# A two-layer transformer kernel on one core: an order planned in finer steps, a key projection moved ahead, and two copies moved from VectorE to ScalarE

## The reference, cut to what matters

```
x = x + L0_attn(layernorm(x))   # one head of 64, biases, causal softmax, output projection
x = x + L0_ffn(layernorm(x))    # 8-bit quantised x and weights, one 256 x 256 product, bias
x = x + L1_attn(layernorm(x))   # 16 heads of 16, rotary positions, causal softmax, projection
x = x + L1_ffn(layernorm(x))    # see below
```

```
xr = mu_r * x + (1 - mu_r) * x_prev
xk = mu_k * x + (1 - mu_k) * x_prev
out = sigmoid(xr @ W_r.T) * (square(relu(xk @ W_k.T)) @ W_v.T)
```

## Time and profile before

| | |
|---|---|
| median of 3 runs | 2519.56 us (2517.97 to 2519.94) |
| profiled execution | 2517.27 us |
| its span in the trace | 2514.1 us |
| PE busy | 2320.8 us (92%) |
| PEld busy | 1053.0 us (42%) |
| DVE busy | 1985.3 us (79%) |
| ACT busy | 1512.4 us (60%) |
| POOL busy | 525.7 us (21%) |
| mean granted clock of PE | 0.981 |

### The profile page before, as it was taken

One profiled execution on the slowest core, in us unless ns is written; L12 is line 12 of the kernel. 1 busy time (PEld: TensorE's weight loads), 2 busy tenths in 40 slices (PEclk: granted clock), 3 DMA queues, 4 the chain that ended last, 5 costly groups with the idle time before them and its releaser, 6 DMA issues.

```text
span 2514.1 us, 52353 instructions
## 1 busy us (share of the span) xinstructions
PE 2320.8 (92%) x19371; PEld 1053.0 (42%) x19371; DVE 1985.3 (79%) x4326; ACT 1512.4 (60%) x2753; POOL 525.7 (21%) x526
## 2 busy tenths in 40 slices
PE   8889899999999899998999999999999999999998
PEld 4544333333434335353444534344344434332345
DVE  5778689887787887879787787997788688899932
ACT  2234456575655666676675666657566577677762
POOL 5453210302215012120403303031121400000011
PEclk9899999999999999999999999999999999999999
DMA  2322220120211312021121302112021121110111
GB/s 56 83 72 73 76 58 25 38 59 18 83 34 35 82 43 73 15 79 29 42 65 37 91 19 76 40 35 78 12 76 35 42 70 45 31 42 27 28 37 36
DMA packets 185896, 125.41 MB, mean 50 GB/s; under 512 B 84912, under 2 KB 185392, under 8 KB 185648
## 3 DMA queue, kind: packets, MB, share of 16 engines
q1 hardware_dynamic: 184880, 121.16, 17.4%
q10 hardware_dynamic: 768, 0.92, 0.1%
HBM read 62.20 MB, written 59.24 MB: 48 GB/s over the span
## 4 chain that ended last, share of the span: by engine, by line
PE 55%; DVE 29%; ACT 6%; issue 4%; DMA 2%; SPq 2%; DVEq 1%; POOL 1%; POOLq 0%; ACTq 0%
DVE mx L1543 20%; PE psum L1867 12%; PE psum L1845 6%; PE psum L1812 6%; PE psum L1778 4%; ACT probs L1303 4%; PE psum L1742 3%; PE psum L1887 2%; PE psum L1713 2%; PE psum L1898 2%; PE psum L1651 2%; PE psum L1918 2%; PE psum L1799 2%; PE psum L1906 2%; DVE stats L1402 1%
## 5 line engine op out<-in xcount | busy, mean ns | idle before, releaser
L1303 ACT ACTIVATE probs<-psum 128x512 f32<-128x512 f32 x2176 | 1139.4, 607 | 465.8 <-PE psum L1845 310.2
L1543 DVE TENSOR_REDUCE mx<-psum 128x1 f32<-128x512 f32 (+2 forms) x2304 | 1283.4, 620 | 140.9 <-PE psum L1812 99.5
L1867 PE MATMUL psum<-probs,vs 128*17 128x512 f32 (+3 forms) x5120 | 590.7, 543 | 0.7 <-ACT probs L1303 0.3
L1812 PE MATMUL psum<-kst,qst 48*128 48x512 f16 (+3 forms) x2560 | 439.6, 354 | 71.0 <-DVE mx L1543 37.7
L1845 PE MATMUL psum<-qst,kst 50*128 50x512 f16 (+3 forms) x2560 | 428.7, 353 | 55.7 <-DVE mx L1543 19.5
L1812 PEld LDWEIGHTS psum<-kst,qst 48*128 48x128 f16 x2560 | 134.0, 94 | 397.5 <-DVE mx L1543 154.5
L1845 PEld LDWEIGHTS psum<-qst,kst 50*128 50x128 f16 x2560 | 128.2, 94 | 360.1 <-ACT probs L1303 131.4
L1867 PEld LDWEIGHTS psum<-probs,vs 128*17 128x17 f32 x5120 | 93.1, 96 | 155.5 <-issue 127.6
L1088 POOL TENSOR_SCALAR vare<-mv 128x4 f32<-128x4 f32 x64 | 15.5, 241 | 595.5 <-DVE mv L1405 595.5
L1819 PE MATMUL psum<-maskq,identh 64*128 64x128 bf16 (+1 forms) x2048 | 131.1, 205 | 0.0
L1117 POOL TENSOR_TENSOR sums<-probs 128x512 f32<-128x512 f32 x12 | 15.3, 1272 | 494.3 <-ACT probs L1257 494.3
(11 more groups left out here) (173 smaller groups left out, 2876.2 us busy)
## 6 DMA issues: line engine op xcount, KB each, us to landing
qk_dram<-parts SPq DMA_DIRECT2D x168, 128.0 KB
qst<-qk_dram SPq DMA_DIRECT2D x128, 96.0 KB, 2.3
kst<-qk_dram SPq DMA_DIRECT2D x128, 96.0 KB, 2.3
v_dram<-vst SPq DMA_DIRECT2D x64, 136.0 KB, 4.0
vs<-v_dram SPq DMA_DIRECT2D x64, 136.0 KB, 2.1
xs<-x_in SPq DMA_DIRECT2D x16, 512.0 KB, 3.5
x_dram<-xs SPq DMA_DIRECT2D x16, 512.0 KB, 2.9
att_dram<-ast SPq DMA_DIRECT2D x64, 128.0 KB, 2.0
```

The costliest lines, as they stand in the source:

```text
L1303: act.activation(dst, src, ACT.Exp, scale=DK1 ** -0.5 / LIFT ** 2).then_inc(S["exp"], 1)
L1543: ins = dve.tensor_reduce(mx1[:, n % 2, 2 * g + odd, tile % TPC, c:c + 1], bank(src, at, at + cols), AX.X, ALU.max)
L1812: ins = pe.matmul(two[odd][:, at:at + cols], qst[rows, qslot, pair, P * (tile % TPC):P * (tile % TPC + 1)], kst[rows, kslot, pair, 0:cols] ...
L1867: ins = pe.matmul(bank(7, off, CH, rows=VW, row=32 * h), vtile[:, h, :], probs[:, HG * (step_no(b, hg, k) % PSTEPS) + h, at:at + CH - off] ...
```

## The change

Four things change. The planner's stretch goes from 40 to 25 us and its drawings from 8 to 16, and each drawing is played to three stretches ahead (75 us) in place of two (80 us). In the tail, the mix for K comes before the mix for R, and K before R. The copy of the turned maxima, `turnmax d`, goes from DVE to ACT, with 0.2 us for it in the plan in place of 0.13. The copy of the first attention's values, `v0`, goes from DVE to ACT, with the same 0.4 us in the plan. Since every queue comes from the plan, the order of all the other work changes too.

```diff
-STRETCH, WAYS, MOVE = 40.0, 8, 10.0
+STRETCH, WAYS, MOVE = 25.0, 16, 10.0
...
-                self.go(trial, then, number, (at + 2) * STRETCH, weights)
-                rank = (max(trial.free_at["PE"], (at + 2) * STRETCH) - trial.work, way)
+                self.go(trial, then, number, (at + 3) * STRETCH, weights)
+                rank = (max(trial.free_at["PE"], (at + 3) * STRETCH) - trial.work, way)
...
-    add("DVE", "v0", c, key(), 0.4, ("V0", c), free=("V0", c))
+    add("ACT", "v0", c, key(), 0.4, ("V0", c), free=("V0", c))
...
-        add("DVE", "turnmax d", me, end - 20, 0.13, ("turnmax", me), ("rows", block_before(b, hg, q, 2)),
+        add("ACT", "turnmax d", me, end - 20, 0.2, ("turnmax", me), ("rows", block_before(b, hg, q, 2)),
             free=("turnmax", me))
...
-    for i in range(2):
+    for i in (1, 0):
         add("ACT", "prod", (*c, i), key(), 1.2, *both(3), ("carry", c),
...
         add("DVE", "mix", (*c, i), key(), 1.33, ("prod", (*c, i)), *both(3))
-    for n in range(2):
-        add("PE", "R", (*c, n), key(), 1.71, ("mix", (*c, 0)), lat=0.1, claim="P", mode="F")
-        add("ACT", "gate", (*c, n), key(), 0.5, ("R", (*c, n)), ("addv", p and (*p, n)),
-            lent and (("FFN", lent) if n else ("scores0", (*lent, TPC * NQ // 2 - 1))), free=("R", (*c, n)))
     for n in range(2):
         add("PE", "K", (*c, n), key(), 1.71, ("mix", (*c, 1)), lat=0.1, claim="P", mode="F")
...
         add("POOL", "sq", (*c, n), key(), 1.04, ("relu", (*c, n)))
+    for n in range(2):
+        add("PE", "R", (*c, n), key(), 1.71, ("mix", (*c, 0)), lat=0.1, claim="P", mode="F")
+        add("ACT", "gate", (*c, n), key(), 0.5, ("R", (*c, n)), ("addv", p and (*p, n)),
+            lent and (("FFN", lent) if n else ("scores0", (*lent, TPC * NQ // 2 - 1))), free=("R", (*c, n)))
...
+                    act.activation(nmaxT1[:, n % 2, :], home("turnmax", item).bitcast(F16)[0:32, 0:P],
+                                   ACT.Copy).then_inc(S["turnmax d"], 1)
...
+                    act.activation(v0[:, TPC * q:TPC * (q + 1), :],
+                                    tiles(home("V0", item)[:, 0:TPC * DK0], DK0), ACT.Copy).then_inc(S["v0"], 1)
...
-                    dve.tensor_copy(v0[:, TPC * q:TPC * (q + 1), :],
-                                    tiles(home("V0", item)[:, 0:TPC * DK0], DK0)).then_inc(S["v0"], 1)
...
-                    dve.tensor_copy(nmaxT1[:, n % 2, :], home("turnmax", item).bitcast(F16)[0:32, 0:P]
-                                    ).then_inc(S["turnmax d"], 1)
```

## The result

The changed kernel takes 2528.38 us (median of 7 runs, 2523.80 to 2530.18) against 2519.52 us for the kernel before (7 runs): ratio 1.0033, 95% interval 1.0021 to 1.0045. It is slower by 8.9 us, where 18 us less were forecast, and above the range given.

What follows compares the result with a forecast made beforehand. The prediction held the kernel bound by how tightly five fixed-order queues mesh on TensorE, VectorE second. Key projection −3.8, copies −4.2 and finer order −10 summed to −18.0 us: 2501.6 us against the 2519.56 median, range 2475 to 2525.

Steps and rivals of the forecast that it cites:

- finer order: Planner's order of all five queues: more drawings, shorter stretches; −10 us, a quarter of the gain, between −42 and +16.
- the windows of one execution: Attention windows per batch: loss bounded at +16 us if batches 1 and 2 fall to batch 3's 91.5% useful TensorE time.
- Key projection first: Two exposed tails at the end: K before R closes the 1.88 us hole before V in each, −3.8 us.
- The copies: Turned maxima and first values move from VectorE to ScalarE: 5.7 us won, 1.5 us paid, −4.2 us.
- The slow one: Rival: the new order is worse in batches 1 and 2, as planner's costs aren't the chip's; 2532 us, chance 0.13.
- Nothing but the end moves: Rival: order luck is zero and freed VectorE time becomes waiting; only −3.8 us, 2515.8 us, chance 0.16.
- VectorE is the bound: Rival: the copies' 50.4 us count in full, 2455 us, or busy time alone, 19.8 us, 2486 us; chance 0.19.

Runs made afterwards that it cites:

- e13: Changed kernel's own plan kept, both copies put back into VectorE's queue by planned start: ratio to the kernel before 1.0084, 2539.0 us.
- e5: Kernel before planned anew with only the planner's three numbers changed (stretch 25 us, 16 drawings, three stretches ahead): ratio 0.9982.
- e7: Kernel before planned anew with the old planner's numbers, only the copies of the turned maxima moved to ScalarE: ratio 0.9946.
- e6: Kernel before planned anew with the old planner's numbers, only the key projection first in all sixteen tails: ratio 1.0038.
- e8: Kernel before planned anew with the old planner's numbers, only the copies of the first values moved to ScalarE: ratio 1.0064.
- e4: Order of the kernel before kept up to the last two tails, which alone do the key projection first: ratio 0.9977, 2513.3 us.
- e3: Plan of the kernel before kept, both copies moved to ScalarE's queue by planned start: ratio 0.9973, 2511.2 us.

## Why the prediction was wrong

**The step that failed is the finer order**, forecast at −10 us between −42 and +16. The order that came out costs 0.84% (0.67 to 1.02), some 21 us, when the copies are put back on VectorE (e13), and TensorE's useless time rose by 18.4 us between the first copy out and the last. The planner's numbers alone don't lose (e5: 0.9982, 0.9965 to 1.0000); the order that they and the other edits made together does.

Two sentences of the prediction carried the error. It called its case "a better choice within what is there: two more of the same drawings, not a new kind of order": it took the order of before for a usual one that a longer search improves. That order is the best of four drawings of its planner, the fourth level with it, and any edit that makes the plan anew gives it up, for better (e7) or worse (e6, e8). And it bounded the loss by the windows of one execution, 91.5% against 92.95%. Stretches of one order don't show how orders differ: the drawings spread to +48 us. (In that bound, batch 2's part is 6.6 us, not 6.9; the sum stays at 16.) The trace could not show the new order, as the prediction says, but the plan could have been read: it is 7.4 us shorter, less than half of the 18 us forecast, and the chip did not follow even that.

**Key projection first** was right in mechanism and size: V at the end of R, 1.88 us less, twice, and 5.8 us (2.5 to 9.1) on its own in e4. That the fourteen tails before lose nothing is not shown.

**The copies** were right in sign; the term of −4.2 us measured −6.8 us in the kept order, with an interval (3.5 to 10.3) that holds it. ScalarE's durations were 262 and 386 ns, not 292 and 393, and its wait, for which I named what queues behind it, did not outweigh the gain. VectorE's busy time fell by 12.8 us, not by 20, and ScalarE's rose by 18.2, not by 25. Rows for the turned maxima were waited for 2.3 us against 1.3: hardly at all, as forecast. The Trainium skill's rule in "ScalarE: Activation LUTs", Rules for kernel authors, sends relu, max, min, add and mul to VectorE; it does not name copies, to which the prediction stretched it. For the narrow copy the durations agree with it, 262 against 204 ns, for the wide one they don't, 386 against 422 ns, and the move won all the same.

**The rivals.** The slow one had the sign, and its price, 2532 us, lies near the 2528; I gave it 0.13. Its reason, that the plan's costs are not the chip's, is borne out by the 18.9 us between plan and chip, and in one place by SyncE's queue, where 2.0 us were planned and 7.6 us passed. Its place was half right: batch 1 lost 8.2 us, but batch 2 won 2.0, and batches 0 and 3 lost 7.0 and 5.3. "Nothing but the end moves" is refuted by e3. "VectorE is the bound" is too: 6.8 us is far from 50.4 us, and from 19.8. The section of the Trainium skill that the prediction set beside this rival, "Perfetto Trace Analysis", Identifying the Most-Contended Engine, asks for TensorE's share of its peak rate besides its weight-load time; the prediction took the second alone, and the engine that it then names, VectorE at 79%, was not the bound here.

What stays open is why one plan is met by the chip and another not, and how a slow order's waits for VectorE, ScalarE and DMAs feed each other. The DMA waits are 9.5 of the 12.8 us here, but they are a count, not an experiment.

## What to carry to other kernels

Where a planner with random choices makes the order, a measured kernel is one drawing, and the one that was kept may be a good one: price an edit in the kept order first, then measure several drawings with and without it, and forecast a new plan with their spread. Read the planner's own length of each plan as well, and how far the chip lies behind it; here it ranked the drawings of one planner, but did not compare two planners. Compare each queue's planned times with the trace, that of the DMA issues too; whether a plan with mended times gives a faster kernel was not tried. An engine's wait in front of a moved instruction is no cost until someone behind it is shown to be late.

## What the runs showed of the hardware that was not expected

In the stretch shown of the changed kernel one DMA issue occupies SyncE's queue for 0.57 to 0.74 us, and twelve in a row hold it for 7.6 us; those of 2 KB (L937: two in 1.35 us) take no less than those of 128 KB (L952). A ScalarE copy of 32 x 128 elements out of PSUM takes 262 ns, where an exponential of 128 x 128 took 292 ns. Raising the mean granted clock from 0.981 to 0.988 by more fill did not change the time (0.9994, 0.9980 to 1.0007).
